# Expert stage of a decoder layer: four staging buffers for the weighed rows, stores of normalised chunks placed elsewhere in SyncE's order, last load in halves

## What is computed

```python
scores = softmax(xf @ Wg.T);  weights, experts = top_k(scores, 2);  weights /= weights.sum(-1)
h1 = xf @ W1[e].T + low_rank + b1;  h3 = xf @ W3[e].T + low_rank + b3
y_e = (silu(h1) * h3) @ W2[e].T + low_rank + b2
y = sum over a token's two experts of weight * y_e
x = layernorm(x + y)
```

## Time and profile before

| | us |
|---|---|
| runs, median | 1248.8 |
| lowest, highest of three | 1245.96, 1255.19 |
| profiled execution, run | 1265.7 |
| its span | 1263.9 |
| busy in the span: TensorE | 1185.1 (94%) |
| VectorE | 852.9 (67%) |
| ScalarE | 790.0 (63%) |
| GpSimd | 773.2 (61%) |

### The profile page before, as it was taken

The page is one execution under the profiler, slowest core; times in us unless marked ns, Lnnn a source line. Parts: engine busy times, 40 slices in busy tenths (PEclk is TensorE's granted clock), DMA queues, the critical chain, the costliest instruction groups (busy, mean ns, idle before and its releaser), DMA issues.

```text
span 1263.9 us, 28342 instructions
## 1 busy us (share of the span) xinstructions
PE 1185.1 (94%) x10786; PEld 685.3 (54%) x10786; DVE 852.9 (67%) x1548; ACT 790.0 (63%) x952; POOL 773.2 (61%) x512
## 2 busy tenths in 40 slices
PE   7999999999999999999999898689999999999991
PEld 3554233333333333333444443369999999999981
DVE  4456998999899989998468787614445545554551
ACT  4556999999999999998566566122223333232221
POOL 2235788888788888777366977524445455445542
PEclk9999999999999999999999999789999999999996
DMA  7697855595559454462477953657787888887863
GB/s 240 221 339 249 250 89 88 86 273 89 80 97 259 78 77 77 82 131 80 126 182 175 220 175 125 221 210 235 231 256 248 267 263 245 277 263 238 254 198 66
DMA packets 134081, 232.53 MB, mean 184 GB/s; under 512 B 31466, under 2 KB 80399, under 8 KB 133623
## 3 DMA queue, kind: packets, MB, share of 16 engines
q1 hardware_dynamic: 108456, 184.09, 50.1%
q0 software_dynamic: 20864, 35.61, 14.6%
q10 hardware_dynamic: 4622, 10.96, 2.7%
HBM read 103.88 MB, written 52.79 MB: 124 GB/s over the span
## 4 chain that ended last, share of the span: by engine, by line
PE 65%; DVE 17%; issue 6%; DMA 5%; ACT 4%; POOL 2%; another core or an unknown queue 1%; ACTq 0%; SPq 0%; DVEq 0%; POOLq 0%
PE xp_ps_h L2546 18%; PE sa_sum L715 9%; PE sa_o L729 9%; PE xp_ps_y L2556 8%; DVE sa_probs L769 8%; PE qp_ps L319 4%; PE sa_factor L715 4%; DMA y_sum<-stage,xp_place_of 4%; PE qp_ps L346 2%; ACT sa_probs L795 2%; DVE sa_o_out L747 1%; PE cb_misc L1349 1%; PE xp_ps_x L2535 1%; PE cb_misc L1329 1%; PE cb_l L1365 1%
## 5 line engine op out<-in xcount | busy, mean ns | idle before, releaser
L769 DVE TENSOR_TENSOR sa_probs<-sa_sum,sa_strips 128x1024 f32<-128x1024 f32 x352 | 413.2, 1219 | 41.6 <-PE sa_sum L715 40.8
L819 POOL TENSOR_TENSOR sa_probs<-sa_probs,sa_factors 128x1024 f32<-128x1024 f32 x160 | 383.6, 2398 | 92.3 <-ACT sa_probs L789 92.3
L795 ACT ACTIVATE sa_probs<-sa_probs 128x1024 f32<-128x1024 f32 (+1 forms) x256 | 342.7, 1383 | 0.0
L2546 PE MATMUL xp_ps_h<-arena,big 128*128 128x128 f32 x2272 | 267.6, 276 | 5.0 <-ACT arena L2575 3.9
L2546 PEld LDWEIGHTS xp_ps_h<-arena,big 128*128 128x128 f32 x2272 | 265.8, 193 | 11.2 <-ACT arena L2575 5.8
L729 PE MATMUL sa_o<-sa_probs,sa_v 128*17 128x512 f32 x2048 | 264.8, 592 | 0.8 <-POOL sa_probs L819 0.6
L2500 POOL DMA_INDIRECT y_sum<-stage,xp_place_of x71 | 115.0, 1619 | 181.0 <-DMA y_sum<-stage,xp_place_of 56.7
L715 PE MATMUL sa_sum<-sa_qk 97*32 97x512 bf16 x2816 | 200.4, 380 | 11.7 <-DVE sa_probs L769 4.8
L715 PEld LDWEIGHTS sa_sum<-sa_qk 97*32 97x32 bf16 x2816 | 62.9, 95 | 228.7 <-DVE sa_probs L769 130.5
L789 ACT ACTIVATE sa_probs<-sa_factor 128x1024 f32<-128x1024 f32 x160 | 164.2, 1026 | 2.6 <-PE sa_factor L715 1.5
L2585 ACT ACTIVATE stage<-arena,xp_weight_of 128x256 f32<-128x256 f32 x71 | 36.1, 508 | 170.7 <-DVE arena L2636 85.0
(11 more groups left out here) (258 smaller groups left out, 1251.8 us busy)
## 6 DMA issues: line engine op xcount, KB each, us to landing
big<-big SPq DMA_DIRECT2D x142, 512.0 KB
sa_qk<-qstack SPq DMA_DIRECT2D x90, 128.0 KB
sa_qk<-kstack SPq DMA_DIRECT2D x90, 128.0 KB
sa_strips<-line SPq DMA_DIRECT2D x3, 3840.0 KB, 18.0
oT<-sa_o_out SPq DMA_DIRECT2D x32, 256.0 KB, 2.4
kstack<-qp_parts SPq DMA_DIRECT2D x48, 128.0 KB, 3.2
qstack<-qp_parts SPq DMA_DIRECT2D x48, 128.0 KB
sa_factors<-factor_line SPq DMA_DIRECT2D x3, 1920.0 KB, 22.1
```

Source lines behind the costliest of these rows:

```text
L769: nc.vector.tensor_tensor(probs[s % RING][:, 2 * half:2 * half + 2, :], ps_sum[sums_before(s, half) % 2][:, :, :], strips[hg % 2][:, 2 * h ...
L795: nc.scalar.activation(probs[s % RING][:, 0:heads, :], probs[s % RING][:, 0:heads, :], ACT.Exp, scale=0.25).then_inc(exp_done, 1)
L819: nc.gpsimd.tensor_tensor(probs[s % RING][:, 2:4, :], probs[s % RING][:, 2:4, :], factors[hg % 2][:, :, c1 - CH:c1][:, :, ::-1], ALU.mult) ...
L2546: last = nc.tensor.matmul(ps_h[parity % 2][:, n, m * P:(m + 1) * P], w_now[s % WRING][:, n, k, m * P:(m + 1) * P], xT[parity % 2][:, k, :] ...
```

## The change

Weighed rows get four buffers instead of two (all of `stage`), and weigh_out(s) waits for scatter s - 4. The small tiles for statistics, which lay in the other half of `stage`, move to the arena. In SP's loop store_rows(c) now stands at s = 27 + 8c, six tiles behind load_rows(c), instead of store_rows(c - 1) directly ahead of load_rows(c); this concerns chunks 0 to 5. The load of chunk 7 becomes two DMAs of two tiles each, the first counted on `rows_loaded[1]`, the second on `rows_loaded[0]`, and the statistics of the third and fourth tile wait for the second.

```diff
-        y = [stage[:, i * D:(i + 1) * D] for i in range(2)]
-        spare = CrossSpace(stage[:, 2 * D:])
+        YRING = 4
+        y = [stage[:, i * D:(i + 1) * D] for i in range(YRING)]
+        spare = space
...
+            def load_last_rows():
+                for half in range(2):
+                    t = slice(half * TT // 2, (half + 1) * TT // 2)
+                    sp.dma_start(chunk_rows(NCH - 1)[:, t, :],
+                                 io["y_sum"][chunk_of(NCH - 1), :].rearrange("(p t) d -> p t d", t=TT)[:, t, :]
+                                 ).then_inc(rows_loaded[1 - half], 16)
...
             for s in range(NT):
                 c = at(s, last_tile(0) + 7)
                 if c is not None:
-                    if c >= 1:
-                        store_rows(c - 1)
                     load_rows(c)
+                c = at(s, last_tile(0) + 13)
+                if c is not None:
+                    store_rows(c)
...
-            load_rows(NCH - 1)
+            load_last_rows()
             store_rows(NCH - 2)
             store_rows(NCH - 1)
...
-                                        in_=y[s % 2][:, :], in_offset=None, compute_op=ALU.add).then_inc(y_stored[s % 2], 16)
+                                        in_=y[s % YRING][:, :], in_offset=None, compute_op=ALU.add).then_inc(y_stored[s % 2], 16)
...
             def weigh_out(s):
                 act.wait_ge(y_summed, s + 1)
-                if s >= 2:
-                    act.wait_ge(y_stored[s % 2], 16 * (s // 2))
-                nc.scalar.activation(y[s % 2][:, :], y_sum[s % 2][:, :], ACT.Copy, scale=weight_of[:, s:s + 1]).then_inc(y_done, 1)
+                if s >= YRING:
+                    act.wait_ge(y_stored[s % 2], 16 * (s // 2 - 1))
+                nc.scalar.activation(y[s % YRING][:, :], y_sum[s % 2][:, :], ACT.Copy, scale=weight_of[:, s:s + 1]).then_inc(y_done, 1)
...
             def statistics(c):
                 dve.wait_ge(rows_loaded[c % 2], 16 * (c // 2 + 1))
                 for t in range(TT):
+                    if c == NCH - 1 and t == TT // 2:
+                        dve.wait_ge(rows_loaded[0], 16 * (NCH // 2 + 1))
                     last = counted(nc.vector.bn_stats(stats[c % 2][:, t, :], chunk_rows(c)[:, t, :]))
```

## The result

The changed kernel is slower: 1261.63 us, median of 20 runs (1253.89 to 1265.93), against 1257.83 (1245.96 to 1268.83) for 20 runs of the kernel before; ratio 1.0058, interval 1.0037 to 1.0078. Forecast were 1243.7 us and a gain of 5.1. The ratio and its interval are of fast runs alone (those more than 1.5% above the fastest of their kernel are left out), while the medians of all 20 and 20 runs are only 3.8 us, 0.3%, apart. So the loss is small, and it rests on the ratio, on the repetition (e14_changed_again) and on the two kernels further down that differ by the wait.

The account below looks back on a forecast made before the run. It took TensorE's pace of 5.518 us a tile, then the serial scatter chain, as the bound. Four buffers -4.7, stores 0, halved load -0.4 gave -5.1: 1248.8 to 1243.7 us, range 1238 to 1256.

Parts of the forecast that it names:

- Part 1: Weighed rows in the expert stage: four buffers end ScalarE's waits for scatters and bring scatter 70 forward, -4.7 us.
- everything that paces the chain up to scatter 65 is 4.7 us earlier: Scatter chain: it locks to TensorE's weight traffic, so scatter 70 also comes 4.7 us earlier.
- the sign of a wrong forecast that it named itself: End of the expert stage: TensorE's lost 4.7 us come back and the last scatter doesn't move.
- nothing, if the chain alone sets its pace: Scatter chain's end: lower bound of the four buffers' gain, nothing; the other bound was 8.5 us.
- Part 2: SP's loop: store c moved ahead of tile 27 + 8c's weights, which leave 6.0 us late; sum taken as 0.
- a free space of 1.3 us: Tile 27's weights: needing 5.4 us of the 6.7 left, they arrive 1.3 us before hidden(27) needs them.
- I take 0 for the sum: Moved stores and shifted DMA traffic: net cost 0, from -0.6 to +2.7 us a pair on the chain.
- the bound of 2.7: Scatter chain at each moved store: tile 27's megabyte in the burst costs at most +2.7 us a pair.
- Part 3: Tail: last load in halves lets two statistics run while the second half lands, -0.4 us.
- B: Scatter chain: the burst makes it slip a second tile, gathers late, TensorE stalls; +0.4, 1249.2 us, chance 0.27.
- C: Weights of tiles 27 to 67 come late behind SP's wait: 1252.7 us halfway, 1261.1 at the bound, chance 0.15.
- D: Scatter chain: spacing works and it is never set back by a tile; -8.9, 1239.9 us, chance 0.10.

Follow-up runs that it names:

- e14_changed_again: The changed kernel run again, nothing altered, on another comparison with the kernel before; ratio 1.0077.
- e1: The kernel before with only the four buffers for weighed rows, stores and last load as before; ratio 1.0003.
- e12: The kernel before with only the four buffers, run a second time; ratio 1.0003.
- e8: The changed kernel with only SP's wait for the normalising at tile 27 + 8c and the store itself at 30 + 8c; ratio to before 1.0056.
- e4: The changed kernel with the stores at tile 30 + 8c instead of 27 + 8c; ratio to before 0.9952.
- e7: The changed kernel storing chunk c - 1 instead of c at tile 27 + 8c, so without the wait; ratio to before 0.9945.
- e2: The kernel before with only the stores moved to tile 27 + 8c, two buffers, whole last load; ratio 1.0114.
- e13_gathers_earlier: The changed kernel with five buffers for x and the gathers one tile further ahead of the scatters; ratio to before 1.0138.
- e10: The changed kernel storing chunk c - 1 at tile 25 + 8c, midway between two loads, without any wait; ratio to before 0.9934.
- e11: The kernel before with only the stores moved to tile 30 + 8c, two buffers, whole last load, no wait of SP; ratio 0.9950.

## Why the prediction was wrong, point by point

**What bounds the stage.** Right: TensorE's pace of 5.518 us, and the serial chain of scatters at the end. In the experiments S is the part of the expert stage that moves most.

**Part 1, -4.7 us for the four buffers.** Wrong, and the step is 'everything that paces the chain up to scatter 65 is 4.7 us earlier'. It made the chain's end follow TensorE. e1 and e12 measure 0 (1.0003 twice; 4.7 us would be 0.9963, just outside both intervals), S is 396.6 and 396.7 with two and with four buffers, each with one late setback, and 390.8 and 390.4 without any. That is the sign of a wrong forecast that it named itself: TensorE's time comes back and the last scatter does not move. The bound 'nothing, if the chain alone sets its pace' was the right value. A second fault lies in the same term: it was read from one profile, 17 us above the median of the three plain runs, and carried over to that median whole. Three profiles of before have L 4.7, 9.2 and 2.7; what one execution loses by a setback that comes by chance is not what the median can give back.

**Part 2, the moved store.** The reading of the code was right, at the first of the six stores to a tenth: the weights 6.0 us late by the forecast, 6.1 measured (the later waits of SP are longer, up to 9.4 us); a free space of 1.3 us before TensorE would wait for them itself, and out(26) came only 0.13 us late. The step that failed is 'I take 0 for the sum', from -0.6 to +2.7 us a pair. It priced only TensorE's own wait and a slightly longer burst. The wait alone costs 13 to 14 us (e8 against e4 and e7), the moved stores alone as much (e2). At the first store the pair of scatters behind 24 took 9.46 + 7.52 = 16.98 us, where before it took 12.81: 4.2 us more, beyond the bound of 2.7. And 16.98 - 2 x 5.52 = 5.9 us is a whole tile at one blow. Two readings led there. The burst of before was taken as the 9 us of the earlier trace rows, from 987 on, and it is 14, from 982 on. And only tile 27's weights were added to it, while those of tile 28, held up by the same wait, leave with them: 970.65 to 975.21, four DMAs.

**Queues.** The Trainium skill ("DMA: Bandwidth & Descriptors", Queues, rings and completion order) says that a DMA engine takes its queues in turn, packet by packet. The forecast concluded from it that a scatter on its own queue would hardly feel SP's backlog, and did not go by that. Rightly: a scatter follows the one before after 4.57 us with no weights moving, and after 8.12 to 9.46 us with the engines full (before, e8, e12, the changed kernel). Whether the engines share as the page says, these runs don't show.

**Part 3, -0.4.** Right in kind, too small: the tail is 15.4 to 16.0 us in the nine profiles with halves and 16.5 to 16.9 in the seven with the whole load, about 1.1 us less.

**The rivals.** B came nearest: the burst, then gathers behind late scatters and turns of x that wait for them. Its second tile did not come in the changed kernel: its sign was a scatter 10 us or more beyond 6.75, and the largest lag is 15.8 us, so the chain was one tile late, only from scatter 26 instead of 48 (e13_gathers_earlier reaches 19.0). B was priced to end at +0.4 us and given 0.27; the change ended at +7 to +10 by the ratios (1.0058 and 1.0077), +4 by the medians of the first comparison. It was priced as one more setback against the full gain of part 1, and that gain wasn't there. That the measured median, 1261.63, lies near the bound of C is chance: 9 us of it are the low median of the three runs of before. C's mechanism was half right: SP's wait is the cause, but it acts mainly through the scatters, and not through weights missing on TensorE (e8 loses nothing in the tiles of the late weights). D has come true in other kernels: the profiles of e4, e7, e10 and e11 have no setback, at S 390.0 to 390.8 (390.2 was worked out for it, 398.7 less 8.5).

## What to carry to other kernels

A wait placed in a queue that also issues prefetches is paid by everything behind it: check that what it waits for is done when the queue gets there, and if it is not, store something older (chunk c - 1) or put it some tiles later; here that is the difference between +0.6% and -0.5% (e8 against e7). Where a serial chain sets the end, more buffers beside it free the other engines but don't end the chain sooner; what helped here was to keep the traffic even, so that one slow scatter is not followed by a second. And before a stall from one profile is booked as a gain, see whether the median execution has it at all.

## What the runs showed of the hardware

The chain of scatters has steps. While the weights go at TensorE's pace it keeps one of two distances for many tiles, some 6.5 us behind out or some 12 (scatters 52 to 62 of the first profile of before stay within 12.0 to 14.2), and a disturbance of 2.6 us is caught up (scatter 25 before) while one of 5.9 us in two scatters (25 and 26 of the changed kernel) is not. Size alone does not decide: 3.7 us were caught up in e12_ring_only_again (9.22, then 4.68), and 2.8 us at scatter 48 of before were not, where the next three came 5.8, 6.7 and 6.2 us apart. Scatter 25 came 6.7 to 9.5 us after 24 in every kernel whose store and load go out within a tile or so of each other, whether SP has waited or not; with the store of older rows at tile 27 or 25, away from the load, it was 5.0 us (e7, e10). Two loads of 256 KB in flight were both usable sooner than one of 512 KB: statistics 3.10 us after the issue instead of 4.42.
